# The feed-forward block's down product as two passes of rounded parts, inside an attention kernel of 64 slots a batch

## The chip, the cores and the metric

The kernel runs on one core of one Trainium2 chip. The metric is the device time of one execution in microseconds. TensorE multiplies, VectorE, ScalarE and GpSimd work element by element, and SyncE issues most of the DMAs. The engines run their own instruction streams and meet at semaphores.

## The reference, cut to what matters

Sixteen sequences of 512 rows and 256 columns go through one layer: attention with 16 heads of 16 columns, in which each row keeps only its 31 largest scores, and then a gated feed-forward network with integer weights. Both are followed by a residual sum and a layer norm.

```python
scores = jnp.einsum('bhqd,bhkd->bhqk', Q, K) / math.sqrt(D)
thresh = top_k(scores, 31)[..., -1:]
scores = jnp.where(scores < thresh, -jnp.inf, scores)
context = einsum('bhqk,bhkd->bhqd', softmax(scores), V)
x = layernorm(x + context @ Wo.T + bo)
gate, up = x @ (w_gate / 127).T, x @ (w_up / 127).T      # 256 -> 768
x = layernorm(x + (silu(gate) * up) @ (w_down / 127).T)  # 768 -> 256
```

## The kernel before, in words

Each of the 16 batches has 64 tiles of scores (16 heads by 4 tiles of 128 rows), and the kernel walks through 64 *slots* a batch, one tile a slot. Every engine has a function `slots` in which the order of its work is written out by hand. A tile passes through stages that lie some slots apart: TensorE makes its scores (slot n, L651), VectorE evacuates them (L934), ScalarE makes two counting passes over them (L492, L502), TensorE writes them again with a penalty (`below`, L661, L662, L664), VectorE sorts the largest out of four blocks (L941, L954 to L961), every eight tiles a threshold is picked (L972 to L996) and checked (slots 1, 9, 17, ... 57), GpSimd makes a mask (L1219, slot n+17), TensorE makes the transposed scores with the mask added (`turned`, L681, L684, slot n+23), ScalarE exponentiates them (L510) and TensorE multiplies by the values (`values`, L698, every second slot). SyncE stacks the split queries and keys of each head with eight DMAs (L385, L386).

Between these stages, one PSUM bank, `bench`, serves all other products one after the other, at slots that tables at the head of the file set. In the slots of batch b the network of batch b-1 is computed: 15 batches' networks run so, inside slots 27 to 63, and the last batch's runs in a tail behind the loops. In a slot the semaphore `ready` says that a product lies in the bench and `taken` that it was read.

The network's rows are held transposed. `x1T` (two tiles) holds its input as a rounded part and the rest; `wg` and `wu` hold the weights' integers in the rounded format (F32R). For each of six parts f of 128 inner values:

- TensorE, slot 42, 44, 46, 49, 51 or 53 (`GATE_SLOTS`): `widen(wg, f)`, L734, four passes of 512 columns into the bench. ScalarE, one slot later, takes its tanh into `th[:, f % 2]` (L542), and VectorE multiplies (L1096, in place, also reads the bench).
- TensorE, the slot after (`UP_SLOTS`): `widen(wu, f)`. ScalarE copies it, scaled, to the single tile `ups` (L547), one slot later, and GpSimd multiplies `th` by `ups` into `hT[:, f]` (L1253), behind the mask of that slot, and counts in `h_done`. The next up copy waits for this product, and the tanh of part f waits for the product of part f-2.

At slots 59 to 62 (`DOWN_SLOTS`) TensorE multiplies 128 rows each: `narrow(t)` (L740) has six products of 256 columns, `hT` (F32) by `wd` (F32, weights times 1/127). An F32 product is recorded as two passes, so a group has 12. VectorE adds the residual in the slot after (L1043) ahead of the evacuation and takes row statistics behind it (L1049, L1052). GpSimd makes the layer norm's factors at slot 63 and ScalarE applies them (L515) at slots 1 and 2 of the next batch.

The integers are loaded once, by five DMAs of `load_network` (L369 to L378) with `wo` and `brow`, into `hT` and `wd`, and GpSimd converts them (L1265 to L1268) before its first mask.

Of the kernel before, what the change touches and what calls it, by code (L numbers as in the profile page):

```python
# [10 lines left out]
HID = 768  # L11
# [69 lines left out]
DOWN_SLOTS = {59: 0, 60: 1, 61: 2, 62: 3}  # L81

# [76 lines left out]
def build(nc, xT, x, wqT, wkT, wvT, woT, bq, bk, bv, bo, wgT, wuT, wdT, ident_in, blocks_in, heads_in, ranks_in, out):  # L159
    with ExitStack() as ctx:  # L160
# [17 lines left out]
        ones = sb("ones", [1, P])  # L178
# [10 lines left out]
        wd = sb("wd", [P, NF, DM])  # L189
# [14 lines left out]
        msq = sb("msq", [P, NT * HALF])  # L204
# [5 lines left out]
        rsd = sb("rsd", [P, NT * HALF])  # L210
# [25 lines left out]
        hT = sb("hT", [P, NF, L])  # L236
# [11 lines left out]
        left = sb("left", [P, 2, BLOCKS * 8])  # L248
        best = sb("best", [P, 2, PAIR, RANKS])
        other = sb("other", [P, PAIR, RANKS])  # L250
        picked = sb("picked", [P, PAIR, RANKS])
        least = sb("least", [P, PAIR])
        hidden = sb("hidden", [P, PAIR])
# [4 lines left out]
        mask = sb("mask", [P, MASKS, NT, L], BF16)  # L258
        PT = sb("PT", [P, 4, L])
# [53 lines left out]
        h_done = sem("h_done")  # L313
        out_done = sem("out_done")
# [44 lines left out]
        def _(sp):  # L359
# [9 lines left out]
            def load_network():  # L369
                sp.dma_start(wo[:, :, :], woT.rearrange("(c p) n -> p c n", p=P)).then_inc(ffn_loaded, 16)  # L370
                sp.dma_start(brow, bo.rearrange("(a n) -> a n", a=1)).then_inc(ffn_loaded, 16)

                for i, src in ((0, wgT), (1, wuT)):
                    sp.dma_start(hT[:, 3 * i:3 * i + 3, :].bitcast(I32).rearrange("p a (c n) -> p (a c n)", c=2)
                                  .rearrange("p (c n) -> p c n", c=C), src.rearrange("(c p) n -> p c n", p=P)
                                  ).then_inc(ffn_loaded, 16)
                sp.dma_start(wd[:, :, :].bitcast(I32), wdT.rearrange("(c p) n -> p c n", p=P)).then_inc(ffn_loaded, 16)
# [63 lines left out]
        def _(act):  # L441
# [76 lines left out]
            def slots(b, first, rest, finish):  # L518
                for n in range(TILES):
# [8 lines left out]
                    for what, part in uses:  # L528
# [9 lines left out]
                        if what == "gate":  # L538
                            act.wait_ge(ready, use + 1)
                            if part > 1:  # L540
                                act.wait_ge(h_done, (b - 1) * NF + part - 1)
                            nc.scalar.activation(th[:, part % 2, :], bench[:, :], ACT.Tanh, scale=0.5 * DEQ).then_inc(th_done, 1)  # L542
                        if what == "up":
# [3 lines left out]
                            nc.scalar.activation(ups[:, :], bench[:, :], ACT.Copy, scale=0.5 * DEQ * DEQ).then_inc(taken, 1)  # L547
# [41 lines left out]
            for f in range(NF):  # L589
# [8 lines left out]
                nc.scalar.activation(ups[:, :], up[:, :], ACT.Copy, scale=0.5 * DEQ * DEQ).then_inc(last_ups, 1)  # L598
# [715 lines left out]
```

## Time and profile before

| | us |
|---|---|
| median of 3 runs | 2994.08 |
| the three runs | 2985.15, 2994.08, 2994.3 |
| the profiled execution, its own time | 3002.92 |
| its span, first to last instruction | 3001.1 |
| TensorE busy, share of the span | 2705.3, 90% |
| VectorE | 2499.2, 83% |
| ScalarE | 2478.7, 83% |
| GpSimd | 2385.7, 79% |
| mean granted TensorE clock | 0.959 of 2.4 GHz |

The names in the profile are PE (TensorE's matmuls), PEld (its weight loads, which overlap them), DVE (VectorE), ACT (ScalarE), POOL (GpSimd) and SPq (SyncE's queue). L740 is line 740 of the kernel. Matmuls are pipelined and each is shown with its latency, so the distance between two starts tells more than a duration; the same holds for the other engines, whose instructions overlap a little. Where the text cuts a batch into slots, slot n begins when VectorE starts the evacuation L934 of tile n.

### The profile page before, as it was taken

To read this page: it belongs to the slowest core of one execution; us is meant where nothing else is said; L and a number is where in the kernel's file an instruction comes from. 1 tells how busy PE (TensorE), PEld (TensorE's weight loads), DVE (VectorE), ACT (ScalarE), POOL (GpSimd) and SP (SyncE) were. 2 spreads that over 40 slices of the span, in tenths; PEclk is the share of its full clock that TensorE was granted. 3 is DMA by queue.
4 is the path that set the end of the run, shared out by engine and by line. 5 is a ranking of instruction groups with operands and counts; after the bars stand their busy time and mean duration, and the time that the engine had idled before them with its cause. 6 is when DMAs were issued, how large, how long until landed. Compare 5 with 4: busy or idle time off the path is not lost.

```text
span 3001.1 us, 81706 instructions
## 1 busy us (share of the span) xinstructions
PE 2705.3 (90%) x21375; PEld 1449.9 (48%) x21375; DVE 2499.2 (83%) x12312; ACT 2478.7 (83%) x5890; POOL 2385.7 (79%) x1668
## 2 busy tenths in 40 slices
PE   5889999989998988899999999999988999899897
PEld 2444544545454444454545455454444545455455
DVE  5888888888889878888898988878888888888883
ACT  4888898888898877888888988878978888888883
POOL 1887888888798876787888888787877879778783
PEclk7899999999999989899999999999999999999998
DMA  3201111020111101111011110211101111110100
GB/s 88 48 21 42 25 41 38 24 49 26 37 30 36 42 21 37 29 29 45 23 42 25 41 39 24 47 27 37 30 25 45 26 40 27 32 42 23 37 2 22
DMA packets 91162, 102.67 MB, mean 34 GB/s; under 512 B 34529, under 2 KB 52962, under 8 KB 90594
## 3 DMA queue, kind: packets, MB, share of 16 engines
q1 hardware_dynamic: 89874, 96.35, 13.4%
q8 instruction: 186, 3.05, 0.5%
q14 instruction: 382, 3.13, 0.4%
q10 hardware_dynamic: 720, 0.14, 0.0%
HBM read 20.86 MB, written 8.39 MB: 10 GB/s over the span
## 4 chain that ended last, share of the span: by engine, by line
PE 36%; DVE 18%; SPq 15%; issue 13%; POOL 8%; ACT 6%; DMA 2%; DVEq 1%; ACTq 0%; POOLq 0%
SPq L386 8%; SPq L385 7%; DVE cand L941 7%; POOL mask L1219 6%; PE bench L740 5%; PE Y_ps L664 5%; PE ST_ps L684 4%; PE Y_ps L661 3%; PE ctxT_ps L698 3%; DVE S L934 3%; PE bench L734 3%; PE bench L605 3%; PE Y_ps L662 3%; PE ST_ps L681 3%; ACT junk L492 2%
## 5 line engine op out<-in xcount | busy, mean ns | idle before, releaser
L1219 POOL TENSOR_SCALAR mask<-S,thr,mb 128x512 bf16<-128x512 f32 x1015 | 2098.4, 2080 | 44.1 <-POOL mb L1213 33.5
L941 DVE MAX8 cand<-Y_ps 128x8 f32<-128x128 f32 x4096 | 1072.0, 282 | 7.4 <-issue 6.9
L492 ACT ACTIVATE junk<-S,at_zero,slope 128x512 bf16<-128x512 f32 x1024 | 824.7, 805 | 99.3 <-DVE S L934 99.2
L934 DVE TENSOR_SCALAR_CACHE_REDUCE S<-S_ps,na 128x512 f32<-128x512 f32 x1024 | 755.9, 738 | 170.7 <-PE S_ps L651 153.2
L502 ACT ACTIVATE above<-S,s,steep 128x512 bf16<-128x512 f32 x1024 | 824.6, 805 | 0.6
L510 ACT ACTIVATE PT<-ST_ps 128x512 f32<-128x512 f32 x1024 | 595.9, 582 | 193.0 <-PE ST_ps L684 187.4
L661 PE MATMUL Y_ps<-ones_b,nbig 128*128 128x512 bf16 x1024 | 403.0, 394 | 169.6 <-DVE cand L941 155.9
L651 PE MATMUL S_ps<-KS,QS 64*128 64x512 f32 x1024 | 523.0, 511 | 4.5 <-DVE S L934 2.3
L664 PE MATMUL Y_ps<-KS,QS 64*128 64x512 f32 x1024 | 523.0, 511 | 0.0
L684 PEld LDWEIGHTS ST_ps<-nbig,mask 128*128 128x128 bf16 x4096 | 235.8, 99 | 382.0 <-issue 382.0
L684 PE MATMUL ST_ps<-nbig,mask 128*128 128x128 bf16 x4096 | 414.8, 225 | 0.0
L681 PE MATMUL ST_ps<-QS,KS 64*128 64x512 f32 x1024 | 412.7, 403 | 0.5 <-POOL mask L1219 0.5
L664 PEld LDWEIGHTS Y_ps<-KS,QS 64*128 64x128 f32 x1024 | 192.1, 188 | 453.7 <-issue 453.7
L662 PE MATMUL Y_ps<-above,nbig 128*128 128x512 bf16 x1024 | 400.0, 391 | 0.0
L698 PE MATMUL ctxT_ps<-PT,V 128*32 128x128 f32 x8192 | 338.9, 284 | 0.1
L1211 POOL TENSOR_SCALAR rbig<-rmax 128x8 f32<-128x8 f32 x128 | 31.1, 243 | 375.9 <-DVEq L1027 375.5
L661 PEld LDWEIGHTS Y_ps<-ones_b,nbig 128*128 128x128 bf16 x1024 | 99.8, 97 | 318.5 <-issue 252.1
L954 DVE MAX8 best<-cand 128x8 f32<-128x32 f32 x1024 | 192.6, 188 | 44.6 <-issue 39.9
L698 PEld LDWEIGHTS ctxT_ps<-PT,V 128*32 128x32 f32 x8192 | 197.2, 111 | 56.2 <-issue 4.3
L681 PEld LDWEIGHTS ST_ps<-QS,KS 64*128 64x128 f32 x1024 | 196.2, 192 | 3.6 <-POOL mask L1219 1.2
L502 ACT ACTIVATION_READ_ACCUMULATOR above<-S,s,steep 128x1 f32 x1024 | 196.7, 192 | 0.0
L492 ACT ACTIVATION_READ_ACCUMULATOR junk<-S,at_zero,slope 128x1 f32 x1024 | 196.1, 192 | 0.0
(187 smaller groups left out, 3684.6 us busy)
## 6 DMA issues: line engine op xcount, KB each, us to landing
QS<-Qhi SPq DMA_DIRECT2D x512, 32.0 KB, 2.0
KS<-Khi SPq DMA_DIRECT2D x512, 32.0 KB, 2.0
KS<-Klo SPq DMA_DIRECT2D x512, 32.0 KB, 2.0
QS<-Qlo SPq DMA_DIRECT2D x512, 32.0 KB, 2.0
xTs<-in_xT SPq DMA_DIRECT2D x17, 512.0 KB, 3.7
xs<-in_x SPq DMA_DIRECT2D x16, 512.0 KB, 3.9
out<-xs SPq DMA_DIRECT2D x15, 512.0 KB, 2.9
hT<-in_wgT SPq DMA_DIRECT2D x1, 768.0 KB
```

The lines of the kernel that those rows point to most:

```text
L492: nc.scalar.activation(junk[:, :], S[:, score_place(j)[0], :], ACT.Tanh, bias=at_zero[:, :], scale=slope[:, hb, col:col + 1], accum_out=s0 ...
L502: nc.scalar.activation(above[:, j % 4, :], S[:, score_place(j)[0], :], ACT.Sign, bias=s0[:, j % 8:j % 8 + 1], scale=steep[:, hb, col:col + ...
L510: nc.scalar.activation(PT[:, j % 4, :], ST_ps[j % 2][:, :], ACT.Exp, scale=SCALE).then_inc(exp_done, 1)
L651: nc.tensor.matmul(S_ps[n % 2][:, :], QS[rows, r, q:q + P], KS[rows, r, :], start=True, stop=True, tile_position=(rows.start, 0)).then_inc ...
L661: nc.tensor.matmul(Y[:, :], nbig[:, :], ones_b[:, :], start=True, stop=False)
L664: nc.tensor.matmul(Y[:, :], QS[rows, r, q:q + P], KS[rows, r, :], start=False, stop=True, tile_position=(rows.start, 0)).then_inc(below_do ...
L681: nc.tensor.matmul(ST[:, :], KS[rows, r, kt * P:(kt + 1) * P], QS[rows, r, :], start=True, stop=False, tile_position=(rows.start, 0))
L684: mm = nc.tensor.matmul(ST[:, t * P:(t + 1) * P], mask[:, h % MASKS, t, kt * P:(kt + 1) * P], nbig[:, :], start=False, stop=(t == NT - 1))
L698: mm = nc.tensor.matmul(ctxT_ps[32 * a:32 * a + 32, strip * P:(strip + 1) * P], V[:, k, grp, strip * VW:strip * VW + 32], PT[:, (j - kt + ...
L934: nc.vector.tensor_scalar(S[:, at, :], S_ps[n % 2][:, :], na[:, hb, col:col + 1], None, ALU.add, op1=ALU.max, accum_out=rmax[:, n % RING:n ...
L941: mx = nc.vector.max(cand[:, j % CANDS, i, :], Y_ps[j % 2][:, i * BW:(i + 1) * BW])
L1219: nc.gpsimd.tensor_scalar(mask[:, h % MASKS, t, :], S[:, score_place(j)[0], :], thr[:, r:r + 1], mb[:, r:r + 1], ALU.is_lt, op1=ALU.add).t ...
```

## The change

The inner values are made in two parts, as the network's input is. GpSimd's product goes to `th` in place instead of to `hT`. ScalarE then copies it into the rounded format (the first part, `h_part(0, f)`), and VectorE subtracts that copy from it (the second, `h_part(1, f)`). The two have slots of their own (`HIGH_SLOTS`, `LOW_SLOTS`) and semaphores (`h_rounded`, `h_split`). `narrow` multiplies both parts by `wd`, which holds the integers in the rounded format; the factor 1/127 goes into ScalarE's scaled up copy. The tanh of part f now waits for the subtraction of part f-2, and the down products for all subtractions. The loads go by way of the mask's tile and `ups`, in six DMAs, and several small tiles are laid over `W`. The tail keeps its F32 products, with `S` for `hT`.

```diff
+HIGH_SLOTS = {45: 0, 47: 1, 49: 2, 52: 3, 55: 4, 56: 5}
+LOW_SLOTS = {46: 0, 48: 1, 51: 2, 53: 3, 56: 4, 57: 5}
...
-        wd = sb("wd", [P, NF, DM])
+        wd = sb("wd", [P, NF, DM], F32R)
...
-        hT = sb("hT", [P, NF, L])
+        hS = sb("hS", [P, 2, NF - 2, L], F32R)
...
+        other, picked = (W[:, i * P:(i + 1) * P].rearrange("p (t r) -> p t r", t=PAIR) for i in range(2))
+        left = W[:, 2 * P:2 * P + 2 * BLOCKS * 8].rearrange("p (a e) -> p a e", a=2)
+        msq, rsd = (W[:, 320 + i * NT * HALF:320 + (i + 1) * NT * HALF] for i in range(2))
+        least, hidden = (W[:, 384 + i * PAIR:384 + (i + 1) * PAIR] for i in range(2))
...
+        def h_part(i, f):
+            return hS[:, i, f, :] if f < NF - 2 else x1T[f - (NF - 2)][:, i, :]
...
+                sp.dma_start(ints[:, 2 * FAN:2 * FAN + 4 * DM].rearrange("p (c n) -> p c n", c=4),
+                             rows[:, 0:4, :]).then_inc(ffn_loaded, 16)
+                sp.dma_start(ups[:, :].bitcast(I32).rearrange("p (c n) -> p c n", c=2),
+                             rows[:, 4:6, :]).then_inc(ffn_loaded, 16)
...
                             if part > 1:
-                                act.wait_ge(h_done, (b - 1) * NF + part - 1)
+                                act.wait_ge(h_split, (b - 1) * NF + part - 1)
...
-                            nc.scalar.activation(ups[:, :], bench[:, :], ACT.Copy, scale=0.5 * DEQ * DEQ).then_inc(taken, 1)
+                            nc.scalar.activation(ups[:, :], bench[:, :], ACT.Copy, scale=0.5 * DEQ * DEQ * DEQ).then_inc(taken, 1)
...
                         normalised(b, 0, X1_SLOTS[n], x1_done)
+                    if not first and not rest and n in HIGH_SLOTS:
+                        f = HIGH_SLOTS[n]
+                        act.wait_ge(h_done, (b - 1) * NF + f + 1)
+                        nc.scalar.activation(h_part(0, f), th[:, f % 2, :], ACT.Copy).then_inc(h_rounded, 1)
...
                 for f in range(NF):
-                    mm = nc.tensor.matmul(bench[:, 0:DM], hT[:, f, t * P:(t + 1) * P], wd[:, f, :],
-                                          start=(f == 0), stop=(f == NF - 1))
+                    for i in range(2):
+                        mm = nc.tensor.matmul(bench[:, 0:DM], h_part(i, f)[:, t * P:(t + 1) * P], wd[:, f, :],
+                                              start=(f + i == 0), stop=(f + i == NF))
...
-                        pe.wait_ge(h_done, b * NF)
+                        pe.wait_ge(h_split, b * NF)
...
+                    if not first and not rest and n in LOW_SLOTS:
+                        f = LOW_SLOTS[n]
+                        dve.wait_ge(h_rounded, (b - 1) * NF + f + 1)
+                        nc.vector.tensor_tensor(h_part(1, f), th[:, f % 2, :], h_part(0, f).bitcast(F32),
+                                                ALU.subtract).then_inc(h_split, 1)
...
-                            nc.gpsimd.tensor_tensor(hT[:, part, :], th[:, part % 2, :], ups[:, :], ALU.mult).then_inc(h_done, 1)
+                            nc.gpsimd.tensor_tensor(th[:, part % 2, :], th[:, part % 2, :], ups[:, :], ALU.mult).then_inc(h_done, 1)
...
-            nc.gpsimd.tensor_scalar(wd[:, :, :], wd[:, :, :].bitcast(I32), DEQ, None, ALU.mult).then_inc(deq_done, 1)
+            flat = wd[:, :, :].rearrange("p c n -> p (c n)")
+            nc.gpsimd.tensor_scalar(flat[:, 0:4 * DM], ints[:, 2 * FAN:2 * FAN + 4 * DM], 1.0, None, ALU.mult).then_inc(deq_done, 1)
+            nc.gpsimd.tensor_scalar(flat[:, 4 * DM:6 * DM], ups[:, :].bitcast(I32), 1.0, None, ALU.mult).then_inc(deq_done, 1)
```

## Rows read from the trace of the kernel before

**Rows 1.** The page's busy times: engine, busy us, share of the span, instructions.

```profile
PE 2705.3 (90%) x21375; PEld 1449.9 (48%) x21375; DVE 2499.2 (83%) x12312; ACT 2478.7 (83%) x5890; POOL 2385.7 (79%) x1668
```

**Rows 2.** The page's chain that ended last, its shares by line.

```profile
SPq L386 8%; SPq L385 7%; DVE cand L941 7%; POOL mask L1219 6%; PE bench L740 5%; PE Y_ps L664 5%; PE ST_ps L684 4%; PE Y_ps L661 3%; PE ctxT_ps L698 3%; DVE S L934 3%; PE bench L734 3%; PE bench L605 3%; PE Y_ps L662 3%; PE ST_ps L681 3%; ACT junk L492 2%
```

**Rows 3.** Busy time by stretch of one batch: TensorE, weight loads, VectorE, ScalarE, GpSimd, clock.

```profile
2495.90:2509.50 13.60, 13.60 (x112) 7.16 (x111) 11.73 (x59) 12.69 (x31) 13.60 (x9) 1.00 0.12 28
2509.50:2529.60 20.10, 20.10 (x167) 11.11 (x167) 17.39 (x84) 19.08 (x45) 19.24 (x13) 1.00 0.12 27
2529.60:2538.40 8.80, 7.37 (x57) 4.26 (x56) 7.86 (x39) 7.11 (x19) 6.39 (x6) 1.00 0.02 6
2538.40:2554.00 15.60, 15.60 (x105) 10.53 (x103) 11.25 (x54) 8.54 (x20) 12.08 (x11) 1.00 0.01 2
```

**Rows 4.** The chain in order of time, same batch: start us, us, what.

```profile
2539.44 0.22 PE Y_ps L661
...
2540.86 0.57 PE ctxT_ps L698 x16
...
2544.22 0.22 PE Y_ps L661
```

**Rows 5.** Groups by line and form: count | busy us, mean ns | idle before.

```profile
L740 PE MATMUL bench<-wd,hT 128*128 128x256 f32 x720 | 170.6, 387 | 0.0
...
L734 PE MATMUL bench<-x1T,wg 128*128 128x512 f32 x360 | 107.3, 419 | 3.3 <-DVE ctxs L1035 3.1
...
L611 PE MATMUL bench<-ident_r,Khi 128*128 128x128 f32 x128 | 21.0, 288 | 0.0
```

**Rows 6.** Timeline of ScalarE, same batch: start us, us, what [idle before].

```profile
2503.90 0.60 ACT L542 ACTIVATE th<-bench 128x512 f32<-128x512 f32 x1 [0.40 <-PE bench L734]
...
2522.40 0.59 ACT L542 ACTIVATE th<-bench 128x512 f32<-128x512 f32 x1
2522.88 0.81 ACT L502 ACTIVATE above<-S,s,steep 128x512 bf16<-128x512 f32 x1
```

**Rows 7.** Timeline of VectorE, same batch, slot 39.

```profile
2482.95 0.69 DVE L1106 TENSOR_TENSOR x1T<-bench,x1T 128x512 fp32r<-128x512 f32 x1 [1.78 <-ACT x1T L551]
2483.56 0.74 DVE L934 TENSOR_SCALAR_CACHE_REDUCE S<-S_ps,na 128x512 f32<-128x512 f32 x1
```

**Rows 8.** Timeline of VectorE, same batch, slots 60 and 61.

```profile
2540.57 0.75 DVE L934 TENSOR_SCALAR_CACHE_REDUCE S<-S_ps,na 128x512 f32<-128x512 f32 x1
...
2544.26 0.42 DVE L1043 TENSOR_TENSOR xs<-bench,xs 128x256 f32<-128x256 f32 x1 [1.15 <-PE bench L740]
2545.15 0.75 DVE L934 TENSOR_SCALAR_CACHE_REDUCE S<-S_ps,na 128x512 f32<-128x512 f32 x1 [0.47 <-PE S_ps L651]
```

**Rows 9.** Timeline of VectorE, same batch, slot 47.

```profile
2504.53 0.69 DVE L1096 SCALAR_TENSOR_TENSOR th<-th,bench 128x512 f32<-128x512 f32 x1 [0.72 <-ACT th L542]
```

**Rows 10.** Durations of one line, then instructions of two other batches from the timeline.

```profile
L972 DVE TENSOR_TENSOR other<-ranks,s x128: 279/292/1174, 63.8 to 2930.8; 128x128 f32<-128x128 f32 x128
...
1259.63 1.29 POOL L1253 TENSOR_TENSOR hT<-th,ups 128x512 f32<-128x512 f32 x1
1259.89 1.17 DVE L972 TENSOR_TENSOR other<-ranks,s 128x128 f32<-128x128 f32 x1
...
2346.88 4.13 POOL L1219 TENSOR_SCALAR mask<-S,thr,mb 128x512 bf16<-128x512 f32 x2
2346.93 0.85 DVE L982 SCALAR_TENSOR_TENSOR picked<-other,best 128x128 f32<-128x128 f32 x1
```

**Rows 11.** Timeline of GpSimd, the batch of rows 3.

```profile
2528.52 1.28 POOL L1253 TENSOR_TENSOR hT<-th,ups 128x512 f32<-128x512 f32 x1
```

**Rows 12.** Another batch: clock of a stretch, then TensorE's timeline.

```profile
1452.40:1455.80 3.40, 3.40 (x12) 2.00 (x11) 3.30 (x16) 1.70 (x6) 3.40 (x2) 0.50 0.01 2
...
1452.20 0.42 PE L661 MATMUL Y_ps<-ones_b,nbig 128*128 128x512 bf16 x1 [1.40 <-DVE cand L941]
...
1457.81 0.38 PE L661 MATMUL Y_ps<-ones_b,nbig 128*128 128x512 bf16 x1
```

More of the change, by code:

```diff
@@ L177, in build @@
         ranks = sb("ranks", [P, RANKS])
-        ones = sb("ones", [1, P])
+        ones = sb("ones", [1, 1])
         ones_3 = sb("ones_3", [3, P], BF16)
@@ L203, in build @@
         nmean = sb("nmean", [P, NT * HALF])
-        msq = sb("msq", [P, NT * HALF])
         var = sb("var", [P, NT * HALF])
@@ L209, in build @@
         sd2 = sb("sd2", [P, NT * HALF])
-        rsd = sb("rsd", [P, NT * HALF])
         rsd2 = sb("rsd2", [P, NT * HALF])
@@ L247, in build @@
         cand = sb("cand", [P, CANDS, BLOCKS, 8])
-        left = sb("left", [P, 2, BLOCKS * 8])
         best = sb("best", [P, 2, PAIR, RANKS])
[L250 to L253, printed above, removed]
         flag = sb("flag", [P, 2, PAIR + 1])
@@ L256, in build @@
         W = sb("W", [P, L])
+        other, picked = (W[:, i * P:(i + 1) * P].rearrange("p (t r) -> p t r", t=PAIR) for i in range(2))
+        left = W[:, 2 * P:2 * P + 2 * BLOCKS * 8].rearrange("p (a e) -> p a e", a=2)
+        msq, rsd = (W[:, 320 + i * NT * HALF:320 + (i + 1) * NT * HALF] for i in range(2))
+        least, hidden = (W[:, 384 + i * PAIR:384 + (i + 1) * PAIR] for i in range(2))
         gtop = sb("gtop", [P, 4, 8])
         mask = sb("mask", [P, MASKS, NT, L], BF16)
+        ints = mask[:, :, :, :].rearrange("p m t l -> p (m t l)").bitcast(I32)
+        FAN = C * HID
         PT = sb("PT", [P, 4, L])
@@ L313, in build @@
         h_done = sem("h_done")
+        h_rounded = sem("h_rounded")
+        h_split = sem("h_split")
         out_done = sem("out_done")
@@ L373, in load_network @@
                 for i, src in ((0, wgT), (1, wuT)):
[L374 to L377, printed above, removed]
+                    sp.dma_start(ints[:, i * FAN:(i + 1) * FAN].rearrange("p (c n) -> p c n", c=C),
+                                 src.rearrange("(c p) n -> p c n", p=P)).then_inc(ffn_loaded, 16)
+                rows = wdT.rearrange("(c p) n -> p c n", p=P)
+                sp.dma_start(ints[:, 2 * FAN:2 * FAN + 4 * DM].rearrange("p (c n) -> p c n", c=4),
+                             rows[:, 0:4, :]).then_inc(ffn_loaded, 16)
+                sp.dma_start(ups[:, :].bitcast(I32).rearrange("p (c n) -> p c n", c=2),
+                             rows[:, 4:6, :]).then_inc(ffn_loaded, 16)
             def stack(h):
@@ L597, in _ @@
                     act.wait_ge(h_done, (B - 1) * NF + f)
-                nc.scalar.activation(ups[:, :], up[:, :], ACT.Copy, scale=0.5 * DEQ * DEQ).then_inc(last_ups, 1)
+                nc.scalar.activation(ups[:, :], up[:, :], ACT.Copy, scale=0.5 * DEQ * DEQ * DEQ).then_inc(last_ups, 1)
             normalised(B, 1, (0, 1), out_done)
@@ L813, in _ @@
             slots(0, True, False)
-            pe.wait_ge(ffn_loaded, 16 * 5)
+            pe.wait_ge(ffn_loaded, 16 * 6)
             pe.wait_ge(taken, FIRST_COUNT)
@@ L820, in _ @@
             pe.wait_ge(brow_loaded, 48)
-            pe.wait_ge(deq_done, 3)
+            pe.wait_ge(deq_done, 4)
             with pe.Fori(1, B, TURN_OF) as b:
@@ L843, in narrow_last @@
                 for t in range(NT):
-                    mm = nc.tensor.matmul(LAST_DOWN[t][:, 0:DM], hT[:, f, t * P:(t + 1) * P], wd[:, f, :],
+                    mm = nc.tensor.matmul(LAST_DOWN[t][:, 0:DM], S[:, f, t * P:(t + 1) * P], wd[:, f, :].bitcast(F32),
                                           start=(f == 0), stop=(f == NF - 1))
@@ L1262, in _ @@
             first_thresholds(0, 0)
-            pool.wait_ge(ffn_loaded, 16 * 5)
+            pool.wait_ge(ffn_loaded, 16 * 6)
             for i, w in enumerate((wg, wu)):
-                nc.gpsimd.tensor_scalar(w[:, :, :].rearrange("p c n -> p (c n)"),
-                                        hT[:, 3 * i:3 * i + 3, :].rearrange("p a n -> p (a n)").bitcast(I32), 1.0, None,
+                nc.gpsimd.tensor_scalar(w[:, :, :].rearrange("p c n -> p (c n)"), ints[:, i * FAN:(i + 1) * FAN], 1.0, None,
                                         ALU.mult).then_inc(deq_done, 1)
-            nc.gpsimd.tensor_scalar(wd[:, :, :], wd[:, :, :].bitcast(I32), DEQ, None, ALU.mult).then_inc(deq_done, 1)
+            flat = wd[:, :, :].rearrange("p c n -> p (c n)")
+            nc.gpsimd.tensor_scalar(flat[:, 0:4 * DM], ints[:, 2 * FAN:2 * FAN + 4 * DM], 1.0, None, ALU.mult).then_inc(deq_done, 1)
+            nc.gpsimd.tensor_scalar(flat[:, 4 * DM:6 * DM], ups[:, :].bitcast(I32), 1.0, None, ALU.mult).then_inc(deq_done, 1)
             slots(0, True, False)
@@ L1278, in _ @@
                 pool.wait_ge(last_ups, f + 1)
-                nc.gpsimd.tensor_tensor(hT[:, f, :], th[:, f % 2, :], ups[:, :], ALU.mult).then_inc(h_done, 1)
+                nc.gpsimd.tensor_tensor(S[:, f, :], th[:, f % 2, :], ups[:, :], ALU.mult).then_inc(h_done, 1)
             layer_norm(B, 1)
```

## The prediction, made before the changed kernel was run

> **What bounds the kernel now.** I read the busy shares first [rows 1]: no engine stands out, so the shares decide nothing. The chain that ended last [rows 2] says the same: it passes from SyncE's queue, which issues the stacking DMAs (15% of the span), to TensorE, VectorE and GpSimd. The kernel is a pipeline of 64 slots a batch whose limit changes from stretch to stretch, so the change has to be priced where its work lies. That is slots 44 to 63, in the 15 batches whose network runs inside the slots (the last batch has a tail of its own, which keeps its products). The stacking DMAs lie in slots 14 to 31; they start when a slot before them has been reached, so they pass on what is gained or lost, and absorb nothing.
>
> I cut one batch at four places, each the start of an evacuation (L934) [rows 3]. In slots 44 to 48 and 49 to 55 TensorE is busy all the time: 13.60 of 13.60 us and 20.10 of 20.10. VectorE has 1.9 and 2.7 us over, ScalarE 0.9 and 1.0. In slots 56 to 58 TensorE idles and VectorE is nearly full, 7.86 of 8.80. In slots 59 to 62, where the down products are, TensorE is full again, 15.60 of 15.60, while VectorE has 4.3 us over, ScalarE 7.1 and GpSimd 3.5. The chain in order of time runs there through TensorE alone: the group for the blocks (L661) begins at 2539.44 in slot 60 and at 2544.22 in slot 61, 4.8 us apart, with 0.57 for the value products between them [rows 4].
>
> **The product.** The change removes 12 fp32 passes of 256 columns in each of four slots and adds 12 passes in the rounded format. Today the 60 groups of 12 keep TensorE busy for 170.6 us [rows 5], 2.84 a group; less the last pass's 0.39 that is 0.22 a pass. No row shows a rounded pass of 256 columns, so I bound it. From below: four rounded passes of 128 columns (L611) take 21.0/32 = 0.66, so (0.66-0.29)/3 = 0.12 each. From above: four rounded passes of 512 (L734) take 107.3/90 = 1.19, so (1.19-0.42)/3 = 0.26 each; a pass of half the columns can hardly take more than today's 0.22, and that, no gain, is the end I keep. Half of 0.26 is 0.13 and the floor is 0.12; the 128-column row is the nearest, and I take 0.12. So 12 x (0.22-0.12) = 1.2 us a slot comes off, 4.8 us a batch, if TensorE alone sets the pace.
>
> It won't quite. VectorE waits 1.15 us for the product and then 0.47 for the scores behind it [rows 8]. These waits go, and when they have gone, VectorE's own work is late next: from evacuation to evacuation 2545.15-2540.57 = 4.58, less the waits 2.96; the next two slots have a step of the picking more, 0.3 (L972's median) [rows 10]. TensorE's slot is 4.78 with the value products and 4.2 without; less 1.2 that is 3.6 and 3.0. VectorE's three slots come to 9.5, TensorE's to 10.2: only some 0.3 is lost to VectorE, in the first of them, where TensorE is ahead. I take **4.5 us a batch**, between 3.5 (a pass of 0.14) and 4.8.
>
> **ScalarE's copies.** Six of 128x512 from SBUF, unscaled. ScalarE's instructions overlap: the tanh starts at 2522.40 and lasts 0.59, but the sign behind it starts at 2522.88 [rows 6], so a 512-column pass occupies it for 0.48. That is from PSUM; from SBUF the nearest is that sign pass (L502), with two column operands, 0.81 less the same overlap = 0.7, the upper end. I take 0.48, as there are no such operands: 2.9 us a batch. TensorE holds the stretch with 5.7 us for two slots (20.10 over seven slots). A copy stands at the end of its slot, ahead of the next slot's up copy or tanh. The tanh is what hurries, since VectorE's gate step and then TensorE's up product, a slot later, wait for it; ScalarE waits 0.40 for the gate product ahead of it [rows 6], so of a copy's 0.48 some 0.1 comes through. The up copy has until the next gate product. I charge 0.2 a batch; without the cover it would be 2.9.
>
> **VectorE's subtractions.** Six, 128x512, two SBUF inputs. The nearest is L1106, the same operation and output with one input in PSUM: it starts at 2482.95 and the evacuation behind it at 2483.56 [rows 7], 0.6 us. Four of them (slots 46, 48, 51, 53) fall where VectorE waits some 0.7 a slot for others [rows 9]: hidden, 0; without that cover 2.4. Those of slots 56 and 57 fall into VectorE's full stretch and delay evacuation and everything behind it: 2 x 0.6 = **1.2 us a batch** on the path. Their new wait for ScalarE's copy is met a slot earlier. The tanh of two parts later waits for the subtraction where it waited for GpSimd's product; it is due a slot after it.
>
> **The shared port.** A subtraction with both inputs in SBUF is of the kind of L972 and L982. L972's median is 0.29, but some take 0.8 to 1.2 [rows 10]. L982 started 0.05 after a mask and took 0.85; L972 started 0.26 into GpSimd's product (L1253) and took 1.17, to just after the product's end. So a mask of 2.08 holds VectorE off only for its first 0.6 us, GpSimd's own two-input product for nearly all its 1.28. The median being clean, most starts miss both. But slot 56's subtraction is due in the last 1.1 us ahead of the evacuation at 2529.60 [rows 3], and GpSimd's product runs from 2528.52 to 2529.80 [rows 11]: up to 0.9 of waiting. I charge 0.6 a batch, between 0 and 1.9 (two full stalls on the path). The Trainium skill, page "SBUF — State Buffer", section "SBUF: two separate sides", says more: the pair of ports is an exclusive lock held for the whole instruction, and the loser blocks fully. For the product the trace agrees; for the mask it doesn't, as 0.85 is far below 2.08. Its consequence is a rival below.
>
> **The rest.** GpSimd's product writes in place: same instruction, no cost. Loading has one DMA and one conversion more for the same bytes, ahead of GpSimd's first mask at slot 17: nothing. The small tiles laid over others change no instruction. Sum: -4.5 + 0.2 + 1.2 + 0.6 + 0.1 for the semaphore steps = -2.4 us a batch, x15 = **-36 us**. The profiled execution took 3002.92 us and would take 2967; the runs' median, 2994.08, lies 0.3% below it and would be 2958. With the bounds it is -3.6 to -0.1 a batch: 2940 to 2993.
>
> **The rivals.**
> - The cover fails (no change): ScalarE is at its limit in slots 44 to 56, so all six copies, 2.9, come on top of 1.2 and 0.6. 4.7 against 4.5: +3 us, 2997. For it: ScalarE is idle for only 0.9 and 1.0 us there [rows 3]. Against: the 0.40 ahead of each tanh takes up most of a copy.
> - The clock falls. TensorE waits 1.40 for VectorE ahead of slot 59, here in another batch [rows 12]; this wait grows by up to 1.2. In one batch of 15 the granted clock was 0.50 (the 1.2 GHz level) just behind this wait, and slot 59's TensorE work took 5.6 (1452.20 to 1457.81) instead of 4.2 (the slot without value products, above). If every batch did so: 1.4 x 15 = 21 back, 2979.
> - Slower: GpSimd holds the port for each whole instruction, at each subtraction. It is busy 79% [rows 1] with instructions of 2.08, so a subtraction waits 0.79 x 1.04 = 0.8 on average and costs 1.4. The two on the path cost 2.8; the four others exceed their 0.7 of cover by 0.7 each, 2.8. With 0.2 for ScalarE 5.8 against 4.5: +1.3 a batch, +20, 3014. It decides from a mean wait of 0.6. For it is L972's 1.17, against it the median of 0.29. The rule of the Trainium skill (page and section named above) would do this here.
> - The change doesn't do what it says: a rounded pass of 256 columns takes the 0.22 of today. No gain, 2.1 of cost: +31, 3025. Against it: L734 does twice the columns in 0.26.
>
> **Chances.** Forecast 0.62, fallen clock 0.11, failed cover 0.11, held port 0.11, no faster pass 0.05. The predicted time is the forecast's. Faster by over 0.3% (about what a measurement here can tell): 0.73; within: 0.11; slower: 0.16. The range leaves the last two rivals out and takes in the others and the forecast's bounds, with the scatter of the runs: 2936 to 3000.
>
> **What would show it.** L740's groups of 12 at 1.6 to 1.7 us, so some 100 us busy in all. Slots 59 to 62, 15.6 now, at 11.1; slots 44 to 56 longer by at most 1; slots 57 and 58 by 0.6. VectorE's wait of 1.15 for L740 gone. The subtraction at 0.7 of duration where no product of GpSimd runs, 1.2 to 1.6 where one does. I am wrong if L740's pace stays above 0.2, if slots 44 to 58 lengthen by more than 3, or if the granted clock falls in most batches behind slot 58.

## The result, and the profile after

The changed kernel took 2976.96 us (median of 6 runs, 2972.46 to 2983.74) against 2990.52 us for the kernel before on the same chip (6 runs, 2985.15 to 2998.82): a ratio of 0.996, interval 0.9947 to 0.9973, or 13.6 us less. In a second comparison, with 10 and 13 runs, it was 2985.39 against 2991.97 us, 0.9973 (0.9963 to 0.9982). So the change is faster, clear of the noise, by 7 to 14 us where the forecast was 36: the sign was right and the size was not.

The profiled execution took 2982.24 us, with a span of 2980.4 us. Its busy times stand against [rows 1]:

```profile
PE 2648.8 (89%) x21375; PEld 1408.9 (47%) x21375; DVE 2551.4 (86%) x12402; ACT 2520.9 (85%) x5980; POOL 2398.8 (80%) x1669
```

TensorE has as many instructions as before and is busy 56.5 us less. VectorE and ScalarE have 90 more each and are busy 52 and 42 us more. What this is worth is seen by stretch, in the same batch and with the same cuts as [rows 3] (L952 is now the evacuation): slots 44 to 48, 49 to 55, 56 to 58, 59 to 62.

```profile
2477.80:2492.20 14.40, 14.01 (x117) 7.44 (x116) 13.40 (x62) 13.93 (x34) 14.40 (x9) 1.00 0.11 25
2492.20:2513.50 21.30, 19.92 (x165) 10.85 (x163) 19.95 (x88) 21.07 (x50) 20.09 (x14) 1.00 0.12 28
2513.50:2522.60 9.10, 7.36 (x57) 4.45 (x56) 8.14 (x40) 6.72 (x18) 5.25 (x5) 0.90 0.01 2
2522.60:2535.20 12.60, 12.60 (x106) 8.43 (x105) 11.09 (x55) 8.55 (x20) 12.27 (x11) 0.94 0.00 1
```

The four stretches were 13.60, 20.10, 8.80 and 15.60 us. The last is 3.0 shorter; the first three are together 2.3 longer. The two stretches that were full on TensorE now have gaps on it (14.01 of 14.40, 19.92 of 21.30), and the granted clock is below 1 behind them, 0.90 and 0.94. Over all 15 batches, cut at every evacuation: slots 44 to 58 went from 647.8 to 681.9 us (+34.1), slots 59 to 62 from 234.9 to 183.6 (-51.3). The difference is -17. The two profiled executions are 20.7 apart; the medians only 13.6, and 6.6 in the second comparison, so some of what the stretches gain does not show in the medians. The first batch, which has no network in its slots, took 176.4 us instead of 173.6. I take the sums and medians "by slot" below from these starts of the evacuation, as the prediction did.

**The product** is as fast as forecast. The chain in order of time gives three groups of 12 passes, in slots 59 to 61; the first fell into a stretch of low clock, the other two did not:

```profile
2521.11 2.67 PE bench L758 x12
...
2526.03 1.61 PE bench L758 x12
...
2529.08 1.50 PE bench L758 x12
```

Before, such a group took 2.84 with its last latency [rows 5]; now 1.68 at full clock, 1.16 less. VectorE's wait for it (the line's list of who waited: engine, tile, line, us, times) fell from the first row, of the kernel before, to the second, of the changed one:

```profile
  DVE xs L1043: 39.4, 46
```

```profile
  DVE xs L1061: 2.0, 11
```

**The subtraction** (L1133) takes 0.67 where nothing disturbs it. One line of min/median/max for each of its output tiles:

```profile
L1133 DVE TENSOR_TENSOR hS<-th,hS x60: 661/673/1267, 324.7 to 2866.8; 128x512 fp32r<-128x512 f32 x60
L1133 DVE TENSOR_TENSOR x1T<-th,x1T x30: 666/673/1649, 352.3 to 2879.8; 128x512 fp32r<-128x512 f32 x30
```

The maxima are not rare. The one of slot 56, part 4, took 1.3 to 1.65 in 14 of 15 batches; the one of slot 46, part 0, took 0.9 to 1.27 in 12. Both are shown here beside GpSimd's work at the time: first VectorE's timeline, then GpSimd's.

```profile
2483.65 1.26 DVE L1133 TENSOR_TENSOR hS<-th,hS 128x512 fp32r<-128x512 f32 x1
...
2511.02 1.64 DVE L1133 TENSOR_TENSOR x1T<-th,x1T 128x512 fp32r<-128x512 f32 x1
```

```profile
2483.59 2.08 POOL L1242 TENSOR_SCALAR mask<-S,thr,mb 128x512 bf16<-128x512 f32 x1
...
2510.83 1.29 POOL L1276 TENSOR_TENSOR th<-th,ups 128x512 f32<-128x512 f32 x1
2512.08 2.52 POOL L1242 TENSOR_SCALAR mask<-S,thr,mb 128x512 bf16<-128x512 f32 x1
```

Slot 46's began 0.06 after a mask of 2.08 and lost 0.6. (In the three other batches it began just as close behind the mask and took 0.67, while the mask took 2.60 to 2.67: there the mask was the one that waited.) Slot 56's began 0.19 after GpSimd's product and ended 0.54 after it: it waited for the whole product. The mask that started during it took 2.52 instead of 2.08, so the wait goes both ways.

**The clock.** TensorE's timeline shows two waits in front of the down products, where there was one of 1.40 [rows 12]:

```profile
2513.34 0.20 PE L730 MATMUL bench<-flag,onesc 128*1 128x9 f32 x2 [1.27 <-DVE var L921]
...
2519.41 0.38 PE L678 MATMUL Y_ps<-ones_b,nbig 128*128 128x512 bf16 x1 [1.71 <-DVE cand L959]
```

The first is new. The check of slot 56 needs the bench, which `var` (L921) frees, and that stands behind the blocked subtraction on VectorE. The second is the old one, 0.3 longer. Behind them the granted clock was at 0.5, the 1.2 GHz level, for a part of slots 57 to 59 in 10 of 15 batches, twice as long in one of them; before it was one batch of 15. Here are three windows of the same batch; the clock is the number after the five engines:

```profile
2519.41:2520.72 1.31, 1.31 (x8) 0.52 (x9) 1.17 (x6) 0.29 (x2) 1.31 (x1) 1.00 0.00 0
2520.72:2524.13 3.41, 3.41 (x18) 2.94 (x16) 3.41 (x20) 2.52 (x6) 3.41 (x3) 0.50 0.01 2
2524.13:2535.20 11.07, 11.07 (x100) 7.38 (x98) 9.56 (x47) 7.02 (x17) 10.74 (x10) 1.00 0.01 1
```

In all ten batches the clock falls 0.1 to 2.6 us before the first pass of the down product (here at 2520.87), so it was not the shorter passes that brought it down. Slots 59 to 62 took 11.51 us in the batches without it and 12.44 in those with it (13.92 in that one), against 15.56 before.

### The profile page after: what moved, and what is told of

Same layout as the page of the kernel before. It is cut to its first block, busy times and chain, and to the rows that moved or that the text cites. A ratio compares the mean times of both kernels' runs of the same rounds, so it can differ in the third digit from the quotient of the medians.

```text
span 2980.4 us, 81958 instructions
## 1 busy us (share of the span) xinstructions
PE 2648.8 (89%) x21375; PEld 1408.9 (47%) x21375; DVE 2551.4 (86%) x12402; ACT 2520.9 (85%) x5980; POOL 2398.8 (80%) x1669
## 4 chain that ended last, share of the span: by engine, by line
PE 35%; DVE 22%; issue 15%; SPq 11%; ACT 10%; POOL 4%; DMA 1%; DVEq 1%; ACTq 0%; POOLq 0%
DVE cand L959 8%; SPq L399 5%; SPq L398 5%; PE Y_ps L681 5%; DVE S L952 4%; PE ST_ps L701 3%; ACT above L515 3%; PE bench L751 3%; PE Y_ps L678 3%; PE ctxT_ps L715 3%; PE bench L758 3%; ACT junk L505 3%; PE bench L622 3%; PE Y_ps L679 3%; PE ST_ps L698 3%
## 5 line engine op out<-in xcount | busy, mean ns | idle before, releaser
L952 DVE TENSOR_SCALAR_CACHE_REDUCE S<-S_ps,na 128x512 f32<-128x512 f32 x1024 | 754.9, 737 | 144.2 <-PE S_ps L668 121.2
```

The source lines that it names most:

```text
L952: nc.vector.tensor_scalar(S[:, at, :], S_ps[n % 2][:, :], na[:, hb, col:col + 1], None, ALU.add, op1=ALU.max, accum_out=rmax[:, n % RING:n ...
```

## The experiments

Each variant changes the changed kernel; ratios are to the kernel before, run on the same chip. The first four were compared with 11 runs of it at a median of 2994.78 us, the next four with 13 at 2991.97, the last two with 9 at 2991.14.

**1. Slot 56's subtraction behind the evacuation** instead of ahead of it.

```diff
-                    if not first and not rest and n in LOW_SLOTS:
+                    if not first and not rest and n in LOW_SLOTS and n not in (56,):
...
                         evacuate(T, n, b, first)
+                    if not first and not rest and n in LOW_SLOTS and n in (56,):
+                        f = LOW_SLOTS[n]
+                        dve.wait_ge(h_rounded, (b - 1) * NF + f + 1)
+                        nc.vector.tensor_tensor(h_part(1, f), th[:, f % 2, :], h_part(0, f).bitcast(F32),
+                                                ALU.subtract).then_inc(h_split, 1)
```

> The subtraction of slot 56 stands behind that slot's evacuation instead of ahead of it; all else as in the changed kernel. Theory A (the port: the subtraction is blocked by GpSimd's product L1276, VectorE stands still for 1.0 us, TensorE for 1.3, and the granted clock falls soon after): its duration goes from 1.64 to about 0.67, slots 55 and 56 together from 8.0 to about 7.2, the clock stays at 1.0 behind slot 58 in nearly all batches, slots 59 to 62 at 11.5 in all. About 0.9 + 0.7 us a batch, so 20 to 25 us faster than the changed kernel. Theory B (the subtractions cost their bulk on a full VectorE, wherever they stand): within 4 us of the changed kernel.

2967.16 us, ratio 0.9916 (0.9903 to 0.9929). VectorE's timeline, then GpSimd's:

```profile
2497.87 0.79 DVE L1147 TENSOR_TENSOR x1T<-th,x1T 128x512 fp32r<-128x512 f32 x1
```

```profile
2496.09 1.28 POOL L1281 TENSOR_TENSOR th<-th,ups 128x512 f32<-128x512 f32 x1
2497.34 2.08 POOL L1247 TENSOR_SCALAR mask<-S,thr,mb 128x512 bf16<-128x512 f32 x1
```

The subtraction now starts 0.5 after GpSimd's product has ended, well into a mask, and takes 0.79. Slot 55 went from 4.73 back to 3.22 (3.19 before the change) and slot 56 from 3.24 to 3.90. Together that is 7.97 to 7.12: **0.85 a batch was the port**. The two subtractions that are left on the path cost 7.12 - 6.13 = 1.0, where 1.2 was forecast. But the granted clock still fell in 10 of 15 batches, which theory A had not expected, and so it gave 10 us under the changed kernel's median where A had 20 to 25: the wait in slot 56 had only shrunk to 0.7, and the one ahead of slot 59 stood at 1.4 to 1.7 in 12 batches and at 2.0 or more in three. The windows are slots 55 and 56, 57 and 58, and 59 to 62:

```profile
2493.98:2501.14 7.16, 6.31 (x57) 3.78 (x57) 6.50 (x34) 7.16 (x19) 5.44 (x4) 1.00 0.12 27
2501.14:2507.05 5.91, 4.32 (x38) 3.07 (x38) 5.24 (x26) 4.29 (x11) 4.18 (x4) 0.84 0.01 3
2507.05:2519.57 12.52, 12.21 (x104) 8.40 (x104) 11.02 (x55) 8.51 (x20) 12.16 (x11) 0.94 0.01 1
```

So the port and the clock are separate losses.

**2. Subtractions of 8 columns.** The remaining columns of the second part keep their first contents (`hS` is filled once with 0.5 ahead of the slots); TensorE multiplies them all the same.

```diff
-                        nc.vector.tensor_tensor(h_part(1, f), th[:, f % 2, :], h_part(0, f).bitcast(F32),
+                        nc.vector.tensor_tensor(h_part(1, f)[:, 0:8], th[:, f % 2, 0:8], h_part(0, f)[:, 0:8].bitcast(F32),
```

> The six subtractions take 8 columns instead of 512 (the rest of the second part is left at its first contents). Theory A (the port): in slot 56 a short one is blocked as long as a long one, duration 1.1 to 1.2 there and 0.17 elsewhere; only the bulk goes, 0.5 us each for the two in slots 56 and 57: 10 to 15 us faster than the changed kernel, and the clock still falls in several batches. Theory B (bulk alone): slots 44 to 58 go back to those of the kernel before but for the copies, about 2 us a batch, 30 us faster than the changed kernel.

2948.08 us, ratio 0.985 (0.9835 to 0.9864). The total is theory B's 30 us, but not by its way: slots 44 to 58 gave back 18 us (681.9 to 663.5) where B had 30, and slots 59 to 62 another 9 (to 174.6), which is the clock. Theory A, with 10 to 15 us, missed the clock; the short subtraction was blocked as it said. Slot 55 went from 4.73 to 3.97, slot 56 from 3.24 to 2.72, and the clock fell in 2 batches only. Those two had waits of 1.53 and 1.44 ahead of slot 59; twelve others had 1.0 to 1.1. Slots 44 to 54 stayed, though: 30.89 in place of 30.92, against 30.50 before the change (13.67 of them in slots 44 to 48 now, and the rest of the loss later). By form (count, busy us, mean ns):

```profile
L1133 DVE TENSOR_TENSOR hS<-th,hS 128x8 fp32r<-128x8 f32 x60 | 16.6, 276 | 0.0
L1133 DVE TENSOR_TENSOR x1T<-th,x1T 128x8 fp32r<-128x8 f32 x30 | 13.2, 439 | 0.0
```

Undisturbed it takes 0.15; the mean of 0.44 comes from slot 56, where it still takes about 0.82 beside GpSimd's product.

**3. Copies of 8 columns**, the same cut for ScalarE's copies; the rest of the first part keeps its first contents, with `hS` filled as in 2.

```diff
-                        nc.scalar.activation(h_part(0, f), th[:, f % 2, :], ACT.Copy).then_inc(h_rounded, 1)
+                        nc.scalar.activation(h_part(0, f)[:, 0:8], th[:, f % 2, 0:8], ACT.Copy).then_inc(h_rounded, 1)
```

> ScalarE's six copies take 8 columns instead of 512 (the rest of the first part is left at its first contents). If the copies are on the path in slots 44 to 50, as the chain through L577 says, those slots lose 0.3 to 0.5 us and the kernel gets 5 to 8 us faster than the changed one. If their cover holds, nothing: within 3 us.

2974.74 us, ratio 0.9928 (0.9911 to 0.9946). The total does not tell the two expectations apart: it is 2 us under the changed kernel's median, and 10 us by the ratios. Slots 44 to 58 sum to 678.4 us instead of 681.9, 0.23 a batch. The median of slots 44 to 54 is 30.86, but it hides two kinds of batches: about half stand at 30.9 and the others at 30.45 to 30.8. So in slots 44 to 54 taking one kind of work away gives back next to nothing in experiment 2 and less than half here. The clock fell behind slot 58 in 9 batches. In four others it fell a little earlier, right behind the wait of slot 56, which was 1.40 to 1.45 there, and cost nothing: slots 59 to 62 stayed at 11.5.

**4. The waits filled.** TensorE makes the transposed scores of slots 56 and 58 three times over, into the same bank.

```diff
-                nc.tensor.matmul(ST[:, :], KS[rows, r, kt * P:(kt + 1) * P], QS[rows, r, :], start=True, stop=False,
-                                 tile_position=(rows.start, 0))
-                for t in range(NT):
-                    ...
+                for _ in range(3 if n in (56, 58) and not first and not rest else 1):
+                    nc.tensor.matmul(ST[:, :], KS[rows, r, kt * P:(kt + 1) * P], QS[rows, r, :], start=True, stop=False,
+                                     tile_position=(rows.start, 0))
+                    for t in range(NT):
+                        ...
```

> TensorE makes the transposed scores of slots 56 and 58 three times over, into the same place, where it stands idle for 1.3 and 1.7 us in the changed kernel. If the fallen clock behind slot 58 is what its idling brings, the clock stays at 1.0 there in nearly all batches and slots 59 to 62 take 11.5 in all of them: 8 to 11 us faster than the changed kernel, at no other cost. If the clock falls for another reason or the repeats are in the way: no gain, 0 to 10 us slower.

2973.38 us, ratio 0.993 (0.9916 to 0.9945). More work for TensorE, and slots 59 to 62 went from 183.6 us to 172.7: 11.51 in every batch, at full clock. The other stretches stayed (slots 44 to 58: 683.9). **The clock's fall costs 11 us.**

**5. The changed kernel once more**, beside the next three.

> The changed kernel itself, once more, beside the variants of it that run on the same chip. All theories: the same time as before, 2970 to 2984 us, about 0.4 to 0.5% under the kernel before, and a granted clock of half behind slot 58 in 8 to 12 of the 15 batches. If its clock falls in another number of batches here, the variants' counts have to be read with that much scatter.

2985.39 us, ratio 0.9973 (0.9963 to 0.9982), above the expected range by a hair. Slots 44 to 58 680.9 us, slots 59 to 62 185.6, the clock fallen in 12 batches. The stretches repeat within 2 us; the two medians of this one kernel differ by 8, so I set a variant's time against the ratio, and its mechanism against the stretches.

**6. Both short**, copies and subtractions of 8 columns (the edits of 2 and 3).

> Copies and subtractions both cut to 8 columns: the product and the order of the waits are left, nearly without the added elementwise work (of the two parts, most columns keep their first contents). Theory A (the added work itself, the subtractions' and then the copies', is what slots 44 to 56 gained, and what let the clock fall): slots 44 to 48 back to 13.6 us, slots 49 to 56 at 23.1 to 23.6 (before 23.0, changed kernel 24.6), slots 59 to 62 at 11.5 with full clock in at least 13 batches, and 2938 to 2946 us in all: a little under the 2948 of short subtractions alone. Rival B (the copies cost nothing, and what is left of the cost is the waits' steps and the port): the same as short subtractions alone within 3 us, 2945 to 2951, and slots 44 to 48 at 13.7.

2948.17 us, ratio 0.9853 (0.9836 to 0.987): the total of short subtractions alone, as rival B had it, but by another way. Slots 44 to 54 are back at 30.48 (13.63 in slots 44 to 48), as in the kernel before, which is theory A: the 0.4 there is the added work (A's total, 2938 to 2946, was missed by 2). By the medians **either kind alone costs nearly all of it** (2: the copies, +0.39; 3: the subtractions, +0.36; both, +0.42). By the means, with the sixth of the 15 batches left out, in which every kernel takes some 9 us more there, it is +0.38, +0.26 and +0.46: the two are less than their sum, and the subtractions alone cost little more than half. Most of that gain is lost again in slot 55, 4.24 here and 3.97 in experiment 2, and with it what is left of the cost, 661.6 - 647.8 = 13.8 us, lies in slot 55 (3.19 before the change). VectorE's timeline there and in slot 56, then GpSimd's:

```profile
2482.27 1.12 DVE L1133 TENSOR_TENSOR x1T<-th,x1T 128x8 fp32r<-128x8 f32 x1
...
2486.04 0.15 DVE L1133 TENSOR_TENSOR x1T<-th,x1T 128x8 fp32r<-128x8 f32 x1
```

```profile
2482.08 1.28 POOL L1277 TENSOR_TENSOR th<-th,ups 128x512 f32<-128x512 f32 x1
```

The same instruction of 8 columns takes 0.15, and 1.12 beside GpSimd's product, ending with it. What it waits for does not depend on its own size.

```profile
2449.50:2463.13 13.63, 13.49 (x110) 7.15 (x111) 12.61 (x61) 12.76 (x33) 13.63 (x9) 1.00 0.11 24
2463.13:2484.22 21.09, 20.05 (x164) 11.12 (x167) 18.62 (x88) 20.29 (x51) 20.25 (x14) 1.00 0.13 28
2484.22:2492.85 8.63, 7.10 (x60) 4.13 (x59) 7.68 (x41) 6.50 (x17) 5.38 (x5) 1.00 0.01 2
2492.85:2504.35 11.50, 10.99 (x98) 7.50 (x100) 10.77 (x54) 8.41 (x20) 11.18 (x11) 1.00 0.01 1
```

**7. The first part's product alone**: six passes a slot; the second part is made and not multiplied.

```diff
-                    for i in range(2):
+                    for i in range(1):
                         mm = nc.tensor.matmul(bench[:, 0:DM], h_part(i, f)[:, t * P:(t + 1) * P], wd[:, f, :],
-                                              start=(f + i == 0), stop=(f + i == NF))
+                                              start=(f == 0), stop=(f == NF - 1))
```

> The down product multiplies the first part alone, six passes a slot; the second part's product is left out. It asks what sets the 11.5 us of slots 59 to 62 at full clock. Theory V (VectorE's own work and the evacuation's step set them, TensorE is no longer late): 11.2 to 11.5 at full clock, so halving the product brings under 0.3 a batch, under 5 us in all; TensorE idles more ahead of and in slots 59 to 62, so the clock falls at least as often (8 to 15 batches) and the total is 2968 to 2985. Theory T (TensorE still sets the pace): 6 passes of 0.12 a slot come off, 11.5 - 2.8 = 8.7 us at full clock, some 40 us in all where the clock stays, 2935 to 2950.

2974.93 us, ratio 0.9937 (0.9915 to 0.9959). Slots 57 and 58, then 59 to 62, of an early batch:

```profile
888.91:894.80 5.89, 4.21 (x35) 2.69 (x35) 5.25 (x27) 3.58 (x10) 4.18 (x4) 0.76 0.01 4
894.80:905.74 10.94, 10.33 (x88) 6.02 (x90) 10.63 (x54) 8.79 (x21) 10.62 (x11) 0.98 0.01 2
```

Half of the passes are gone, some 2.8 us of TensorE a batch, and the stretch shrinks from 11.51 to 10.95. VectorE is now busy 10.63 of 10.94. By slot, at full clock, 59 to 62 were 2.13, 2.82, 3.11, 3.45 and became 2.13, 2.78, 3.11, 2.93: only the last was still TensorE's. Theory V holds in kind, though its size (under 0.3) was too small by half. The clock fell behind slot 58 in 13 batches, but only the 4 in which it stayed low twice as long grew by it, one by 0.5 and three by 1.5 to 1.65: TensorE, with half of the passes, is no longer what the others wait for.

**8. Slot 58 alone filled** (experiment 4 with `n in (58,)`).

> The transposed scores are made three times over in slot 58 alone, so that the wait ahead of slot 59 is filled, while the one in slots 55 and 56 (some 1.1 us) stays. Theory A (the clock falls behind the sum of both waits, and taking away either is enough): full clock behind slot 58 in at least 13 batches, slots 59 to 62 at 11.5, 2970 to 2975 us, as with both filled. Rival B (the wait in slots 55 and 56 is what decides): the clock falls in 8 or more batches as in the changed kernel, 2974 to 2984. With the earlier variant, whose wait in slot 56 shrank to 0.7 and whose clock still fell in 10 batches, A says the wait ahead of slot 59 decides.

2973.22 us, ratio 0.9934 (0.9914 to 0.9954), 12 us under the changed kernel run beside it. Full clock in all 15 batches, slots 59 to 62 at 11.51 and 172.7 in sum. TensorE's timeline and the windows of slots 56 to 58 and 59 to 62:

```profile
2520.13 0.38 PE L678 MATMUL Y_ps<-ones_b,nbig 128*128 128x512 bf16 x1 [0.20 <-DVE cand L960]
...
2523.81 0.38 PE L679 MATMUL Y_ps<-above,nbig 128*128 128x512 bf16 x1 [0.60 <-DVE cand L960]
```

```profile
2514.20:2523.36 9.16, 8.61 (x70) 4.95 (x69) 8.20 (x40) 6.96 (x18) 5.29 (x5) 1.00 0.01 2
2523.36:2534.88 11.52, 11.00 (x98) 7.50 (x100) 10.79 (x55) 8.42 (x20) 11.20 (x11) 1.00 0.01 1
```

The wait of 1.71 is 0.20, and that is enough; the wait in slots 55 and 56 was left (0.91 to 1.27 in 14 batches). With experiment 1 this says that the wait ahead of slot 59 decides. Its length is not all: before the change nearly as long a wait, 1.40, brought the clock down once in 15, and in the changed kernel two of the three batches with the longest waits there (2.1, 2.3 and 2.4) kept full clock. What else enters was not tried. The rows also show where the product's gain ends: TensorE, faster now, waits 0.60 for VectorE in slot 60.

**9. Both repairs**: experiments 1 and 8 together.

> Both repairs at once: slot 56's subtraction behind the evacuation, and the transposed scores of slot 58 made three times over. Theory A (the port and the clock are two separate losses, 0.9 us a batch and 0.9 us in 10 of 15 batches): slots 49 to 56 at 20.3 and slot 56 at 3.9, slots 59 to 62 at 11.5 in all batches, 2955 to 2962 us. Rival B (they are one loss: with the subtraction moved, the refilled slot 58 collides with the next transposed scores or the exponentials, and gives back what the clock gives): slots 57 and 58 longer by 0.5 or more, 2965 to 2972.

2964.66 us, ratio 0.9901 (0.9884 to 0.9918). By stretch, all is as theory A had it: slots 49 to 55 at 20.12, slot 56 at 3.89, slots 57 and 58 unchanged at 5.91, slots 59 to 62 at 11.51 in all batches. Slots 44 to 62 sum to 843.7 us against 865.5 in the changed kernel. The total came out 3 us above A's range, at the foot of B's, though slots 57 and 58 did not lengthen as B had it: slots 31 to 43, which the edit does not touch, had 560 us against 547. In the four kernels with filled waits they had 551 to 562, in the seven other variants of the change, itself included, 544 to 552, and 555 in the kernel before. Whether the clock takes back there a part of what it gives behind slot 58 is open.

**10. Slot 46's subtraction moved too**, behind its evacuation.

> The same with slot 46's subtraction moved behind its evacuation as well. Theory A (the 0.4 us that slots 44 to 48 gained come from that subtraction's start beside a mask, 0.9 to 1.26 us instead of 0.67): the subtraction at 0.67 to 0.70, slots 44 to 48 back to 13.6 to 13.7, 5 to 6 us less than the kernel with slot 56's moved alone, 2949 to 2957. Rival B (they come from VectorE having 0.67 more to do in a stretch without room, port or not): slots 44 to 48 stay at 13.9 to 14.0, within 2 us of the other kernel.

2957.35 us, ratio 0.9886 (0.9871 to 0.9902). VectorE's timeline in slot 46, then the four windows:

```profile
2468.36 0.69 DVE L1148 TENSOR_TENSOR hS<-th,hS 128x512 fp32r<-128x512 f32 x1
```

```profile
2461.89:2476.06 14.17, 14.17 (x117) 7.63 (x117) 13.09 (x62) 13.71 (x33) 14.17 (x9) 1.00 0.12 26
2476.06:2495.99 19.93, 19.41 (x160) 10.62 (x160) 18.26 (x86) 19.59 (x47) 18.86 (x14) 1.00 0.12 26
2495.99:2505.76 9.77, 8.92 (x79) 5.10 (x70) 8.81 (x42) 8.37 (x21) 6.24 (x5) 1.00 0.04 8
2505.76:2517.26 11.50, 11.28 (x100) 7.50 (x100) 10.78 (x54) 8.41 (x20) 11.18 (x11) 1.00 0.01 1
```

The subtraction is down to 0.69 in all 15 batches, as A said, and slots 44 to 48 stay (211.4 us in sum against 212.0), slots 44 to 54 too (30.89): B, the port is not what they lose by. Part 1's subtraction now meets a mask in 9 batches (0.9), but in the six batches in which neither is held up slots 44 to 48 take 13.94 as well, 0.33 more than before the change. Slots 44 to 62 sum to 842.7 us, as in 9, so the 7 us between the two medians are not this edit's; the intervals overlap. These two are the best versions: 1.0 to 1.1% under the kernel before, where the change as it was has 0.3 to 0.4%.

## Why the prediction was wrong

Its parts, a batch, against what the runs showed:

| | forecast | measured | from |
|---|---|---|---|
| product, slots 59 to 62 at full clock | -4.5 | -4.05 | 15.56 to 11.51 |
| slots 44 to 54: six copies, four subtractions | +0.2 | +0.4 | 30.50 to 30.92 |
| subtractions of slots 56 and 57 | +1.2 | +1.0 | 1 |
| port | +0.6 | +0.85 | 1 |
| semaphores | +0.1 | not seen apart | |
| clock | 0 | +0.73 | (183.6 - 172.7)/15 |

The added work sums to 2.25, and the stretch lengthened by 34.1/15 = 2.27. With that, -4.05 + 2.27 + 0.73 = -1.05 a batch or -16 us, for -36 (by the medians -14 and -7). The 20 us between are 11 of the clock, 7 of the product, and 2 to 3 of the added work.

**The step that failed most** is the clock, and it was a choice of chances. The prediction named the mechanism, the place and the price (a rival, 0.11, "1.4 x 15 = 21 back, 2979") and took full clock for its sum. What happened was that rival, at two thirds of its price per batch (0.93 for 1.4; the group behind the wait is shorter now, which I take to be why) and in most batches. The sign that it was likelier stood in the text: a wait of 1.40 had already brought the clock down once in 15 [rows 12], and my own two subtractions stood on VectorE ahead of the instruction that TensorE waits for. The wait grew to 1.7, and the fall came in 10 batches of 15 and in 12 of 15. I treated "one batch of 15" as the odds, where it showed how near the edge the kernel stood. That the port's wait would make a second TensorE wait, by way of `var` and the bench, I did not trace at all.

**The product's term.** The pass was right (0.12; a group 1.68), the group's gain 1.16 for 1.2. Four groups give 4.64, and 0.60 of it is lost where TensorE waits for VectorE in slot 60 (experiment 8), which leaves 4.04; I had put 0.3 for that loss. The cause is the one named, VectorE late next, as experiment 7 shows.

**The port.** Where I charged it, it was there: slot 56, by GpSimd's product, for nearly all of it. I took 0.6 for "up to 0.9"; the start falls 0.19 after the product's in this batch, and it cost 0.85. The page "SBUF — State Buffer" of the Trainium skill, section "SBUF: two separate sides", has the port pair held for the whole instruction. For the product this case agrees: 512 columns took 1.64 instead of 0.67 and 8 columns 1.12 instead of 0.15, both to the product's end. For the mask it does not: 1.26 for a subtraction that began with a mask of 2.08, and 0.69 to 0.82 for those that began later in one. So the rival that held the port for every instruction fell.

**The cover in slots 44 to 54.** The four subtractions there were put at 0 and the six copies at 0.2. Together they cost 0.4. The price is small, but the reasoning behind it was not sound: I gave each kind a cover of its own (VectorE's 0.7 in slot 47 [rows 9], ScalarE's 0.40 ahead of a tanh [rows 6]), and the runs show one cover, of which the copies alone use up nearly all and the subtractions alone more than half. TensorE, full there before, now waits 0.39 in slot 46 in some batches and 0.45 to 0.9 in slot 49 in the others. Here is its timeline, in the changed kernel and then in experiment 2, where the copies are alone:

```profile
2487.57 1.20 PE L751 MATMUL bench<-x1T,wu 128*128 128x512 f32 x4 [0.39 <-DVE th L1114]
```

```profile
2467.30 1.20 PE L751 MATMUL bench<-x1T,wu 128*128 128x512 f32 x4 [0.53 <-DVE th L1114]
```

The first row is slot 46's wait and the second slot 49's; each time the up product waits for VectorE's gate step. In slot 49 that step is late because a copy stands ahead of the tanh: VectorE waits for the tanh there, 0.4 to 1.0 us in most batches. In slot 46 VectorE waits for nobody ahead of the step, and is late itself, behind a subtraction. A batch that lost 0.39 in slot 46 lost 0.11 more in slot 49 or nothing; one that lost nothing in slot 46 lost 0.45 or more in slot 49. With copies and subtractions both short (experiment 6) the wait is gone. So the two kinds meet in this wait, as far as the traces can show it. In experiment 10, with slot 46's subtraction moved, slot 46's wait is gone and slot 49's is 0.51 to 0.53 in 14 of 15 batches, and nothing was gained: the port it is not. The rival in which all six copies come on top (0.11) fell.

**Loading** was put at nothing; the first batch took 176.4 us for 173.6, and 173.2 to 176.8 in the variants, and I did not try to part this from scatter.

Of the marks set, the groups (1.6 to 1.7) and the wait for them were met, and the subtraction's 0.7 and 1.2 to 1.6. The groups' busy time in all was 109 us and not 100, since ten of the 60 ran in part at the low clock. The low end of the forecast's sum, -3.6, leaves the copies and the semaphore steps out; with them it is -3.3. Slots 59 to 62 at 11.1 were 11.5 at full clock. "44 to 56 longer by at most 1, 57 and 58 by 0.6" was placed wrongly by the text's own cut: what stands ahead of an evacuation belongs to the slot before, so slots 55 and 56 took 1.54 and 0.30, and 57 and 58 nothing. And "the granted clock falls in most batches behind slot 58" was the mark for being wrong, and it came.

## What to carry to other kernels

Ahead of a TensorE stretch that matters, list its waits before the change and what the change adds to the engine it waits for. If such a wait has brought the clock down even once, price the fall in the sum and not as an accident; a few matmuls repeated in the wait can buy it back (here 12 us for three times one product). Two-input VectorE work with both inputs in SBUF goes where GpSimd's two-input product does not run: moving one such instruction by one place gained 0.85 us a batch. And two additions on different engines of one pipeline may share one cover (here +0.38 and +0.26 alone, +0.46 together): price them together.

## What was not expected of the hardware

- An 8-column subtraction takes 0.15 us alone and 1.12 beside GpSimd's two-input product: the block does not scale with the blocked instruction. It goes the other way too: a mask that started during a blocked subtraction of 512 columns took 2.52 instead of 2.08.
- GpSimd's mask, one SBUF input with per-partition scalars, blocks VectorE's subtraction for some 0.6 of its 2.08 us only.
- Adding matmuls made the kernel faster: slots 59 to 62 took 11.51 us at full clock in 15 of 15 batches with the wait of 1.71 ahead of them filled, and 12.44 in 10 of 15 with it idle.
- Behind a wait of 1.7 the clock fell in 10 to 12 batches of 15, behind one of 1.5 with 0.7 in slot 56 in 10, and behind one of 1.4 in 1 (before the change). With short subtractions, the copies short or not (experiments 2 and 6), it fell in 2 of 15 each, and those had waits of 1.4 to 1.5 and of 1.9; in the 24 batches with a wait of 1.0 to 1.2 it never fell. A long wait need not do it: some of 2.0 to 2.4 left it at 1.00.
- With six passes a slot instead of 12 the clock falls at the same place and in more batches, and costs nothing in most of them, since TensorE is then not the engine that the others wait for.
